# Order of the first transfers of an expert layer: five weights then six rows, instead of by turns

## The reference

```python
gout = xt @ Wg.T
topv, topi = jax.lax.top_k(gout, 2)            # 2 of 8 experts for each of 4096 tokens
w = jax.nn.softmax(topv, axis=-1)
g = xt @ W1[e].T + b1[e]; v = xt @ W2[e].T + b2[e]
eo = (silu(g) * v) @ W3[e].T + b3[e]           # weighted by w and summed over the two experts
```

## Time and profile before

| | us |
|---|---|
| median of three runs | 798.44 |
| lowest and highest run | 796.09, 801.66 |
| span of the profiled execution, first to last instruction | 798.9 |
| attention 0 | 0 to about 262 |
| routed layer 0, first transpose to last block | 275.8 to about 412 |
| attention 1 | about 412 to 626 |
| routed layer 1, first transpose to last matmul | 630.2 to 780.7 |

### The profile page before, as it was taken

One profiled execution on the slowest core, in us unless ns is written; L12 is line 12 of the kernel. 1 busy time (PEld: TensorE's weight loads), 2 busy tenths in 40 slices (PEclk: granted clock), 3 DMA queues, 4 the chain that ended last, 5 costly groups with the idle time before them and its releaser, 6 DMA issues.

```text
span 798.9 us, 15795 instructions
## 1 busy us (share of the span) xinstructions
PE 702.2 (88%) x5200; PEld 521.8 (65%) x5200; DVE 470.9 (59%) x1335; ACT 331.4 (41%) x683; POOL 393.8 (49%) x516
## 2 busy tenths in 40 slices
PE   4999999999898698888978799999999699999990
PEld 2566666666666497778876455555554399999990
DVE  2566877787677477676556766676564223323325
ACT  2344445444332322222212566666664244444440
POOL 4213276557467345555561266555545245455451
PEclk9999999999997799999997999999999899999996
DMA  6811121111002646767754000000001767777769
GB/s 159 260 12 9 10 36 21 28 27 35 23 22 81 190 143 195 204 202 216 218 177 133 1 27 25 21 20 28 28 24 50 214 204 237 232 224 233 230 198 278
DMA packets 101994, 93.31 MB, mean 117 GB/s; under 512 B 53113, under 2 KB 85753, under 8 KB 101305
## 3 DMA queue, kind: packets, MB, share of 16 engines
q1 hardware_dynamic: 85799, 69.48, 31.9%
q0 software_dynamic: 9088, 18.76, 6.7%
q10 hardware_dynamic: 7025, 4.05, 1.9%
HBM read 70.15 MB, written 24.83 MB: 119 GB/s over the span
## 4 chain that ended last, share of the span: by engine, by line
PE 57%; DVE 19%; issue 8%; DMA 4%; POOL 3%; ACT 3%; another core or an unknown queue 3%; SPq 2%; DVEq 0%; POOLq 0%; ACTq 0%
PE pair L1291 30%; PE pair L1579 11%; PE pair L1294 8%; DVE sm L1058 4%; DVE smax L1054 3%; PE pair L1631 2%; PE pair L1397 2%; POOL xs_sorted L509 2%; PE pair L1412 1%; ACT xa L619 1%; DMA xa<-y_tok 1%; PE pair L1332 1%; DMA y_tok<-ysb,xr 1%; PE pair L1328 1%
## 5 line engine op out<-in xcount | busy, mean ns | idle before, releaser
L582 POOL DMA_INDIRECT y_tok<-ysb,xr x156 | 150.8, 967 | 149.9 <-DVE ysb L976 120.9
L509 POOL DMA_INDIRECT xs_sorted<-xa,slot_i x128 | 129.8, 1014 | 95.2 <-DVE slot_i L895 58.9
L1291 PE MATMUL pair<-xT,w_all 128*128 128x256 f32 x624 | 153.8, 391 | 0.0
L1579 PE MATMUL pair<-w_all,hT 128*128 128x128 f32 x936 | 118.5, 277 | 13.8 <-DVE hT L964 12.0
L1579 PEld LDWEIGHTS pair<-w_all,hT 128*128 128x128 f32 x936 | 117.0, 193 | 20.2 <-issue 16.5
L1291 PEld LDWEIGHTS pair<-xT,w_all 128*128 128x128 f32 x624 | 116.7, 197 | 13.5
L757 ACT ACTIVATE hT<-pair,w_all 128x256 f32<-128x256 f32 x156 | 65.3, 470 | 85.2 <-PE pair L1291 82.3
L956 DVE COPY xT<-pair 128x256 f32<-128x256 f32 x78 | 33.0, 423 | 113.4 <-PE pair L1294 102.9
L753 ACT ACTIVATE hg<-pair,w_all 128x256 f32<-128x256 f32 x78 | 32.7, 470 | 102.2 <-PE pair L1291 67.6
L1054 DVE TENSOR_REDUCE smax<-pair 128x8 f32<-128x616 f32 x64 | 50.4, 788 | 31.2 <-PE pair L1291 30.8
L1291 PE MATMUL pair<-xeT_all,w_sh 128*128 128x512 f32 x128 | 68.1, 614 | 0.0
(11 more groups left out here) (191 smaller groups left out, 1096.2 us busy)
## 6 DMA issues: line engine op xcount, KB each, us to landing
w_all<-in_w SPq DMA_DIRECT2D x39, 578.0 KB
w_all<-in_w SPq DMA_DIRECT2D x39, 450.0 KB
xr<-xs_sorted SPq DMA_DIRECT2D x78, 130.0 KB
xa<-y_tok SPq DMA_DIRECT2D x32, 256.0 KB, 5.3
xs_sorted<-in_pads SPq DMA_DIRECT2D x24, 130.0 KB, 4.3
y_tok<-ysb,xr POOLq DMA_INDIRECT x156
xs_sorted<-xa,slot_i POOLq DMA_INDIRECT x128
out<-x_sb ACTq DMA_DIRECT2D x8, 256.0 KB, 3.1
```

Source lines behind the costliest of these rows:

```text
L509: g.indirect_dma_start(xs_dram[l], bass.IndirectOffsetOnAxis(ap=slot_i[:, i:i + 1], axis=0), xa[:, GT * c + j // TOPK, j % TOPK, :], None) ...
L582: g.indirect_dma_start(y_dram[l], bass.IndirectOffsetOnAxis(ap=xr[u % NXR][:, t, P:P + 1].bitcast(I32), axis=0), ysb[u % NYB][:, t, :], None)\
L1291: return mm(out_, l_, r_, start=True, stop=True)
L1579: last = mm(bank[4 + k][:, t * P:(t + 1) * P], hT[k][:, c, t * P:(t + 1) * P], chunk(w, nu + c, P), start=(c == 0), stop=(c == nc_ - 1))
```

## The change

In `routed(l)` on SyncE, for both layers, the loop that issues weights and rows by turns is split in two: first the weights of blocks 0 to 4, then the rows of blocks 0 to 5. Nothing else changes, neither the steps after these eleven loads nor any buffer or wait.

```diff
                 sp.wait_ge(S("blocks_padded"), 16 * 2 * ND)
+                for k in range(NWB):
+                    block_weights(u0 + k)
                 for k in range(AHEAD):
-                    if k < NWB:
-                        block_weights(u0 + k)
                     block_rows(u0 + k)
                 for u in range(u0, u1):
                     if u + NWB < u1:
```

## The result

Nine runs of the changed kernel have a median of 809.01 us, nine runs of the kernel before beside them 801.21 us; the ratio is 1.0091 with a 95% interval of 1.0058 to 1.0124, that is +7.3 us (4.6 to 9.9). The forecast was +5.7 us. (The three runs that the prediction rests on had a median of 798.44 us; the nine lie higher, so the ratio is compared, not 809.0 with 804.2.) The profiled execution spans 805.7 us, 6.8 us more than before.

The account below looks back on a forecast made before the run. TensorE sets the pace, and layer 1's start is bound by the second block's rows landing. Queue 4.8 + clock 0.5 + layer 0 0.4 = +5.7 us, so 798.44 becomes about 804.2 us, range 799 to 810.

Parts of the forecast that it names:

- The base: Whole kernel: the profiled execution takes 798.9 us, 0.5 us above the median of 798.44 us.
- What bounds the start: Head of layer 1: TensorE's start is bound by the landing of the second block's rows (r1), not by any weights.
- Issue times: SyncE, layer 1: r1 is issued 3.4 us later, at 633.64 instead of 630.25; taken as the least possible loss.
- The queue: SyncE's DMA queue, layer 1: rows wait behind three more weight loads, 5.6 us less 0.8 idle, net +4.8 us.
- The clock: TensorE, start of layer 1: the later start may lengthen the work at half clock; +0.5 us, bounds 0 and +1.
- Layer 0: Head of layer 0: rows land about when the bias step lets TensorE start; +0.4 us, bounds 0 and +1.6.
- The earlier weights: Both layers: weights issued sooner gain nothing, since four blocks of compute already hid them.
- Hidden: Rival, chance 0.20: rows needn't wait behind all weights, only issue delay counts; +3.4 us in layer 1, median 801.8.
- Layer 0 pays: Rival, chance 0.12: slow SyncE steps delay layer 0's rows, +1 to +4 us there, median about 807 us.
- The standstills move: Rival, chance 0.08: two of layer 0's unnamed standstills fall away, -8 us against +5.7, about 796 us.

Follow-up runs that it names:

- e4b_short: Weights first in layer 1 only, with the weight loads of its blocks 1 to 4 cut to 260 of 1156 columns, against the kernel before; ratio 1.0017.
- e1_layer0: The new order (weights first) in layer 0 only, layer 1 still by turns, against the kernel before; ratio 1.0008 (0.9991 to 1.0026).
- e2_layer1: The new order (weights first) in layer 1 only, layer 0 still by turns, against the kernel before; ratio 1.0068 (1.0041 to 1.0096).
- e7_same: The kernel before, unchanged, measured against itself; ratio 1.0009 (0.9979 to 1.0039).
- e9_changed: The changed kernel itself (weights first in both layers), run again on another chip against the kernel before; ratio 1.0050 (1.0017 to 1.0083).
- e3_r1_early: Layer 1 only, order w0 r0 r1 w1 and so on, one weight load ahead of the second rows, against the kernel before; ratio 0.9963 (0.9942 to 0.9985).

## Why the prediction was right or wrong

The direction, the size and the place were right: +5.7 us forecast, +7.3 (4.6 to 9.9) measured, the part in layer 1. That the sum comes so near is in part luck, as its terms show.

*The base.* The prediction took the span of 798.9 us for the time of the profiled execution. In the result's profile the time is 1.9 us above the span (807.6 and 805.7), so that execution probably lay some 2 us above the median and not 0.5. The forecast of the median doesn't depend on it: 798.44 + 5.7 = 804.1.

*What bounds the start.* Right: r0 and r1 of layer 1, with TensorE's order making the first product wait for both. One thing was missed. Before, r0 was transposed 2.9 us ahead of r1 and cost nothing. After, they land close together, the second transpose waits for VectorE's copy of the first (the 0.61 us at 641.34 has VectorE as releaser in the timeline), and it is r0 with 1.27 us behind it that sets the start.

*Issue times.* r1 was forecast 7.8 us behind w0 and came 8.4 us behind. But the statement that later issue alone must cost 3.4 us was wrong: it was meant as the lower bound, and e4b_short shows 0.7 us on its chip; for the chip of the result the estimate above is 2.4 us. A load that is issued long before it lands has time to spare, and only what exceeds that is a loss. The 2.84 us of the earlier trace rows beside the 2.05 us that a free queue needs would have taken 0.8 us off the bound, to 2.6.

*The queue.* +4.8 us forecast; from the list to the first product +4.6 on the chip of the result, +4.8 from e1_layer0 to e2_layer1, +4.9 from e7_same to e9_changed (two chips). Counted from w0, as the forecast did, the second transpose of the result's profiles is 5.4 us later (12.68 and 7.31); from the list it is 4.7 us, as w0 went out 0.7 us sooner behind it. The order of service was right. The rate was not: without rows in between the weights run at 382 to 414 GB/s, not 316, so that three loads take 4.5 us, not 5.6. The forecast's rate came from stretches in which SyncE's pace left gaps. The first loads were slower than that (about 240 GB/s beside other stores), and the serial 1.27 us came on top; the errors cancelled, which is luck. The estimate by the figure of the Trainium skill (page "DMA: Bandwidth & Descriptors", section "Specifications"), 358 GB/s, is passed by these stretches; the same page, section "Measured (HBM→SBUF, 128 partitions, SWDGE, issued from GpSimd)", says that about 358 GB/s is what each core gets with both cores of a pair streaming, and has up to 425 GB/s for a core alone, which the 382 and 414 GB/s agree with. It was the wrong figure to take for one core.

*The clock.* +0.5 forecast, and this term was wrong. From the first product to the third it is 7.52 us before and 6.66 us after in the profiles of the result (-0.9), 6.87 and 7.05 us in e1_layer0 and e2_layer1 (+0.2), 8.44 and 7.96 us in e7_same and e9_changed (-0.5). The later start cost nothing by the clock on the mean, it rather gave back 0.4 us, and only one case of three lies within the bounds 0 and +1. (From the first product to the second, 3.84 us in both e7_same and e9_changed, the last difference doesn't show.) At the other end, the standstill of 1.46 us in e3_r1_early left the clock up.

*Layer 0.* +0.4 forecast, 0.0 in the profiles of the result and 1.0008 (0.9991 to 1.0026) in e1_layer0. Right that the bias step covers it.

*The earlier weights.* Right: they gain nothing.

*The rivals.* "Hidden" falls in its premise, since the rows do stand behind the bytes. "Layer 0 pays" falls by e1_layer0 and by the 21.02 us of the result. "The standstills move" has nothing for it: the stretch with layer 0 is 342.25 us before and 342.59 us after, and the standstills differ between chips far more than between orders. The stage of layer 0 in e1_layer0 and in e7_same (columns as in the earlier trace rows), and the longest waits for an unnamed releaser in e7_same (us in total, times, longest):

```profile
268.00:380.00 112.00, 111.77 (x698) 103.20 (x699) 91.52 (x216) 33.24 (x79) 71.64 (x75) 0.99 0.77 230
```

```profile
282.00:420.00 138.00, 121.26 (x700) 107.42 (x698) 88.93 (x214) 32.87 (x79) 71.32 (x73) 0.95 0.63 189
```

```profile
ACT hg L753 <- remote: 25.5, 7, 4.5
...
DVE hT L964 <- remote: 16.1, 5, 4.6
```

On one chip TensorE is busy 111.77 of 112 us of layer 0, with no unnamed wait among its waits; on the other 121.26 of 138 us. That is 26 of the 40 us by which the first group's chip is ahead of the second's.

*What stays open.* The result's +7.3 us lies 3.5 us above the 3.8 us of head that its own profile shows; with e2_layer1 (+5.2) and e9_changed (+4.0) the intervals overlap between 4.6 and 6.7 us, in which the differences of head of 4.9 us also lie (3.8 us on the result's chip lie below). I take the change at about 5 us. Whether more is lost outside the head on some chips wasn't settled.

## What to carry to other kernels

Where a stage starts with several loads in a row, rank them by when the first computation needs them, and reckon for each both when it is issued and when the bytes ahead of it are through: the later of the two, with some 2 us to land, is when it can be used. Here that was 1.6 to 2.3 us for each weight load of 0.59 MB ahead of the rows, all of it on the path. A load that is needed first and is small belongs right behind the one large load that is needed with it (w0 r0 r1 was at least as fast as the kernel before, 0.9963 and 0.9996, and on the two chips clearly faster than weights first). What is needed four blocks later can wait; issuing it sooner gains nothing and can cost all of its transfer time.

## What the hardware showed that I had not expected

The rows on a second queue came no sooner: the DMA engines served one packet of each queue in turn, 153 beside 136 in 2 us, so a queue of 1040-byte packets beside one of 4624-byte packets gets a fifth of the bytes (0.14 of 0.72 MB), and its first packet started about 3 us after the issue. The same kernel took 766.9 us on one chip and 804 to 806 us on two others, with nearly the same mean granted clock (0.950 in e1_layer0, 0.942 in e7_same; 0.99 and 0.95 in layer 0). What differs in the profiles are standstills, of up to 4.6 us in layer 0, in which ScalarE and VectorE wait for an unnamed releaser, and stretches in which SyncE's register steps take 0.7 us each; what causes either isn't shown. The same step of SyncE (L401, the chain of the kernel before) inside and outside such a stretch:

```profile
620.87 0.71 SPq L401
...
627.87 0.26 SPq L401
```

On the slower chips such a stretch delays SyncE's first load of layer 1 too, to 5.3 us behind the list (628.66 - 623.36) against 1.0 us (589.13 - 588.17).
